# A graph-attention layer on one Trainium2 core: the first stage reordered, packing ahead of the first mask, the late h chunks between half pairs, V's first two chunks on GpSimd

## The reference

```
h      = relu(layernorm(x)) @ W.T + b_W
e      = leaky_relu((h @ a1)[:, None] + (h @ a2)[None, :] + b_a, slope 0.2)
scores = where(adj > 0, e, -9e15)
out    = x + softmax(scores, axis=1) @ h
```

## Time and profile before

| | |
|---|---|
| median of 3 runs | 202.64 us (202.4 to 202.82) |
| profiled execution, its span | 200.8 us |
| TensorE matmul busy | 194.9 us (97%), 3183 instructions |
| VectorE busy | 183.0 us (91%) |
| ScalarE busy | 147.9 us (74%) |
| GpSimd busy | 52.4 us (26%) |
| DMA | 75.66 MB, mean 377 GB/s |

### The profile page before, as it was taken

How to read it: one execution, slowest core, us unless ns; L and a number is a source line. 1 busy time by engine, 2 the same in 40 slices (tenths; PEclk the granted TensorE clock), 3 DMA queues, 4 the chain that set the end, 5 groups by cost and what they waited for, 6 DMA issues and landing times.

```text
span 200.8 us, 7230 instructions
## 1 busy us (share of the span) xinstructions
PE 194.9 (97%) x3183; PEld 189.2 (94%) x3183; DVE 183.0 (91%) x265; ACT 147.9 (74%) x192; POOL 52.4 (26%) x66
## 2 busy tenths in 40 slices
PE   7969999999999999999999999999999999999993
PEld 7648889999999999999999999999999999999993
DVE  4779999999998799897999999999999999999745
ACT  2679879898882777689988888899588888996000
POOL 1002479699995010205000000072000000510000
PEclk9999999999999999999999999999999999999999
DMA  5999999999999999999999999999999999997012
GB/s 181 376 417 418 407 403 423 421 418 415 422 432 408 418 423 419 416 421 418 415 419 423 419 418 421 421 411 421 419 418 418 415 421 416 418 383 226 6 43 66
DMA packets 15968, 75.66 MB, mean 377 GB/s; under 512 B 1600, under 2 KB 5952, under 8 KB 7616
## 3 DMA queue, kind: packets, MB, share of 16 engines
q1 hardware_dynamic: 15792, 75.06, 91.7%
q10 hardware_dynamic: 144, 0.13, 0.3%
HBM read 73.08 MB, written 2.11 MB: 374 GB/s over the span
## 4 chain that ended last, share of the span: by engine, by line
PE 91%; DMA 4%; SPq 1%; DVE 1%; issue 1%; POOL 0%
PE ps L836 29%; PE ps L834 29%; PE ps L840 29%; DMA adj_sb<-in_adj_t 4%; PE ps L808 2%; PE ps L798 2%; SPq L268 1%; SPq L273 1%; PE ps L876 1%; DVE mask L476 0%; POOL bad L788 0%; DVE rden L504 0%; DVE rg L510 0%; DVE bad L519 0%; DVE upper L576 0%
## 5 line engine op out<-in xcount | busy, mean ns | idle before, releaser
L834 PE MATMUL ps<-V,w 128*128 128x129 f16 x1024 | 174.3, 221 | 0.0
L836 PE MATMUL ps<-V,w 128*128 128x129 f16 x1024 | 174.3, 221 | 0.0
L840 PE MATMUL ps<-V,w 128*128 128x129 f16 x1024 | 174.3, 221 | 0.0
L379 ACT ACTIVATE mask<-adj_sb 128x1024 bf16<-128x1024 int32 x126 | 125.5, 1056 | 28.6 <-DMA adj_sb<-in_adj_t 28.6
L459 DVE SCALAR_TENSOR_TENSOR w<-g_row,pairs,mask 128x1024 f32<-128x1024 f32 x96 | 120.5, 1320 | 5.5 <-ACT mask L379 3.6
L834 PEld LDWEIGHTS ps<-V,w 128*128 128x128 f16 x1024 | 100.2, 98 | 1.5 <-ACT H L340 0.7
L836 PEld LDWEIGHTS ps<-V,w 128*128 128x128 f16 x1024 | 100.2, 98 | 1.0 <-issue 1.0
L840 PEld LDWEIGHTS ps<-V,w 128*128 128x128 f16 x1024 | 100.2, 98 | 0.0
L459 DVE SCALAR_TENSOR_TENSOR w<-ps,pairs,mask 128x1024 f32<-128x1024 f32 x31 | 37.4, 1267 | 0.0
L785 POOL TENSOR_TENSOR xT<-xT,x_sb 128x512 f32<-128x512 f32 x6 | 11.5, 1932 | 79.8 <-ACT xT L394 79.8
L739 POOL TENSOR_TENSOR x_sb<-x_sb,b_row 128x512 f32<-128x512 f32 x8 | 10.0, 1301 | 0.0
(11 more groups left out here) (93 smaller groups left out, 63.8 us busy)
## 6 DMA issues: line engine op xcount, KB each, us to landing
adj_sb<-in_adj_t SPq DMA_DIRECT2D x64, 1024.0 KB, 10.3
xT<-in_x_t SPq DMA_DIRECT2D x8, 256.0 KB, 7.5
x_sb<-in_x_p SPq DMA_DIRECT2D x3, 512.0 KB, 10.9
g_row<-g_dram SPq DMA_DIRECT2D x1, 1536.0 KB, 10.3
out<-xT SPq DMA_DIRECT2D x3, 512.0 KB, 9.9
x_sb<-in_x_p SPq DMA_DIRECT2D x2, 256.0 KB, 4.2
out<-xT SPq DMA_DIRECT2D x1, 192.0 KB, 3.4
out<-xT SPq DMA_DIRECT2D x3, 64.0 KB, 1.6
```

The lines of the kernel that those rows point to most:

```text
L379: nc.scalar.activation(mask[:, m % MASKS, r], adj_sb[:, m % HELD, r], ACT.Relu, scale=CONNECTED).then_inc(mask_ready, 1)
L834: nc.tensor.matmul(sums[:, bank, a, :], w16[:, m % SLOTS, col:col + P, 1], V[:, jt, 0, 0:NF], start=(jt == 0 and a == 0), stop=False, skip ...
L836: nc.tensor.matmul(sums[:, bank, a, :], w16[:, m % SLOTS, col:col + P, 1], V[:, jt, 1, 0:NF], start=False, stop=False, skip_group_check=True)
L840: last = nc.tensor.matmul(sums[:, bank, a, :], w16[:, m % SLOTS, col:col + P, 0], V[:, jt, 0, 0:NF], start=False, stop=(jt == NT - 1), ski ...
```

## The change

TensorE does the first three pairs in one go behind h chunk 3, then centring 4, and puts the late h chunks and centrings between half pairs of pairs 3 and 4. In the first pair all products with V's high part come before those with its low part. Within every pair the order of the three products of a block becomes high with high, low with high, high with low. ScalarE's and VectorE's lists are put in the matching order; VectorE packs ahead of the first mask and takes some statistics earlier, and no longer makes products or low parts of V. GpSimd makes the low part of V's chunk 0 (`lows`, in two halves, with the high part still by ScalarE's `highs`) and both parts of chunk 1 (`halves(1)`). Loads, their order and the centring are as before. The diff, cut to its core:

```diff
 # ScalarE
                 relu_chunk(3)
-                highs(0)
+                take_chunk(2)
+                highs(0, 2)
                 first_mask()
-                take_chunk(2)
+                highs(2, 4)
+                take_chunk(3)
                 mask_part(1)
-                take_chunk(3)
+                mask_part(2)
+                weights(1)
+                mask_part(3)
                 relu_chunk(4)
-                highs(1)
-                mask_part(2)
+                mask_part(4, (0,))
                 take_chunk(4)
                 relu_chunk(5)
-                weights(1)
-                mask_part(3)
+                mask_part(4, (1,))
                 take_chunk(5)
                 relu_chunk(6)
-                mask_part(4)
+                mask_part(5, (0,))
                 take_chunk(6)
                 relu_chunk(7)
-                mask_part(5)
+                mask_part(5, (1,))
                 take_chunk(7)
                 mask_part(6)
                 weights(2)
 # VectorE
-                early_mask()
+                statistics(2, 5, 8)
                 pack(0)
                 scale_weights(0)
-                products(0)
+                early_mask()
                 dve.wait_ge(pairs_ready, 1)
                 weigh_first(0)
-                lows(0)
                 weigh_first(1)
                 weigh(0, 1)
-                statistics(2, 5, 8)
+                statistics(3, 0, 4)
                 weigh(1, 0)
                 weigh(1, 1)
-                products(1)
-                lows(1)
                 scores(1)
                 weigh(2, 0)
                 weigh(2, 1)
+                statistics(3, 4, 8)
                 pack(1)
                 scale_weights(1)
-                statistics(3)
                 weigh(3, 0)
                 weigh(3, 1)
                 statistics(4)
 # GpSimd
+                def lows(g0, g1):
...
+                    step(nc.gpsimd.tensor_tensor(prod[:, 0, r, :], H[:, r, H0:HC], by, ALU.mult))
+                    pool.wait_ge(high_ready, g1 // 2)
+                    nc.gpsimd.tensor_tensor(V[:, r, 1, 0:NF], prod[:, 0, r, :], V[:, r, 0, 0:NF],
+                                            ALU.subtract).then_inc(low_ready, 1)
+
                 deviations(2, 3)
+                lows(0, 2)
+                lows(2, 4)
+                halves(1)
                 halves(2)
                 halves(3)
 # TensorE
+                def first_pair():
+                    pe.wait_ge(high_ready, 1)
+                    pe.wait_ge(w_begun, 1)
+                    for k in range(GI):
+                        if k == CT:
+                            pe.wait_ge(w_ready, 1)
+                        high_products(0, 0, k)
+                    pe.wait_ge(w_ready, 2)
+                    for k in range(GI):
+                        high_products(0, 1, k)
+                    pe.wait_ge(low_ready, 1)
+                    for side in range(2):
+                        for k in range(GI):
+                            last = low_product(0, side, k)
+                    last.then_inc(mm_done, 1)
...
                 h_chunk(3)
+
+                pe.wait_ge(h_ready, 3)
+                first_pair()
+                whole(1)
+                whole(2)
                 centre_chunk(4)
-
-                pe.wait_ge(h_ready, 3)
-                whole(0)
+                side_of(3, 0)
                 h_chunk(4)
                 centre_chunk(5)
-                whole(1)
+                side_of(3, 1)
                 h_chunk(5)
                 centre_chunk(6)
-                whole(2)
+                side_of(4, 0)
                 h_chunk(6)
                 centre_chunk(7)
-                whole(3)
+                side_of(4, 1)
                 h_chunk(7)
-                for m in range(4, NM - ENDS):
+                for m in range(5, NM - ENDS):
```

More of the change, by code:

```diff
@@ L211, in gat_layer_kernel @@
         ones_ready = sem("ones_ready")
-        product_ready = sem("product_ready")
         high_ready = sem("high_ready")
@@ L361, in weights, with highs, mask_part @@
                                          scale=SLOPE).then_inc(weights_ready, 1)
-                def highs(c):
+                def highs(g0, g1):
                     act.wait_ge(scaled_ready, 1)
                     act.wait_ge(ones_ready, 1)
-                    act.wait_ge(h_ready, c + 1)
-                    for j in range(CT):
-                        g = c * CT + j
+                    act.wait_ge(h_ready, 1)
+                    for g in range(g0, g1):
                         ins = nc.scalar.activation(V[:, g, 0, 0:NF], H[:, g, H0:HC], ACT.Copy, scale=evr[:, g:g + 1])
                     ins.then_inc(high_ready, 1)
-                def mask_part(m):
+                def mask_part(m, sides=(0, 1)):
                     act.wait_ge(adj_loaded[m % HELD], 16 * (m // HELD + 1))
-                    for side in range(2):
+                    for side in sides:
                         if m >= MASKS:
@@ L547, in statistics @@
                         last = nc.vector.bn_stats(stats[:, g, :], x_sb[:, g, :])
+                        if i >= FIRST_SETS and g % CT == CT - 1:
+                            last.then_inc(stats_ready, 1)
                     if i >= FIRST_SETS:
-                        if first + k1 == end:
-                            last.then_inc(stats_ready, 1)
                         return
@@ L586, in scale_weights @@
                     nc.vector.tensor_tensor(evr[:, r], ev[:, r], rstd[:, 2, r], ALU.mult).then_inc(scaled_ready, 1)
[L588 to L601, removed]
                 step_(nc.vector.memset(ramp[:, 0:1], 0.0))
@@ L719, in deviations @@
                     r = slice(SETS[first][0], SETS[end - 1][1])
-                    pool.wait_ge(stats_ready, end - FIRST_SETS)
+                    pool.wait_ge(stats_ready, SETS[end - 1][1] // CT - FIRST_SETS)
                     nc.gpsimd.tensor_tensor(spread[:, 0, r], stats[:, r, 2], stats[:, r, 5], ALU.add)
@@ L735, in add_b @@
                     else:
-                        pool.wait_ge(stats_ready, i - FIRST_SETS + 1)
+                        pool.wait_ge(stats_ready, SETS[i][1] // CT - FIRST_SETS)
                     pool.wait_ge(b_row_loaded, 16)
@@ L746, in halves @@
                     r = slice(c * CT + k0, c * CT + k1)
-                    part = 1 if c < 4 else 2
+                    part = 0 if c < 2 else 1 if c < 4 else 2
                     pool.wait_ge(scaled_ready, part + 1)
@@ L750, in halves @@
                     pool.wait_ge(h_ready, c + 1)
-                    if c < 4:
-                        pool.wait_ge(low_ready, c - 1)
                     by = evr[:, r].rearrange("p (n a) -> p n a", a=1).to_broadcast([P, k1 - k0, NF])
@@ L757, in halves @@
                                             ALU.subtract).then_inc(v_ready, 1)
+                def lows(g0, g1):
+                    r = slice(g0, g1)
+                    pool.wait_ge(scaled_ready, 1)
+                    pool.wait_ge(ones_ready, 1)
+                    pool.wait_ge(h_ready, 1)
+                    by = evr[:, r].rearrange("p (n a) -> p n a", a=1).to_broadcast([P, g1 - g0, NF])
+                    step(nc.gpsimd.tensor_tensor(prod[:, 0, r, :], H[:, r, H0:HC], by, ALU.mult))
+                    pool.wait_ge(high_ready, g1 // 2)
+                    nc.gpsimd.tensor_tensor(V[:, r, 1, 0:NF], prod[:, 0, r, :], V[:, r, 0, 0:NF],
+                                            ALU.subtract).then_inc(low_ready, 1)
                 deviations(2, 3)
+                lows(0, 2)
+                lows(2, 4)
+                halves(1)
                 halves(2)
@@ L811, in h_chunk, with high_products @@
                     last.then_inc(h_done, 1)
-                def products(m, k0, k1):
+                def high_products(m, side, k):
                     group, at = divmod(m, PAIRS)
+                    jt = 2 * at + side
+                    col = side * GC + k * P
+                    bank, a = sums_at(group, k)
+                    nc.tensor.matmul(sums[:, bank, a, :], w16[:, m % SLOTS, col:col + P, 1], V[:, jt, 0, 0:NF],
+                                     start=(jt == 0 and a == 0), stop=False, skip_group_check=True)
+                    return nc.tensor.matmul(sums[:, bank, a, :], w16[:, m % SLOTS, col:col + P, 0], V[:, jt, 0, 0:NF],
+                                            start=False, stop=False, skip_group_check=True)
@@ new lines, in low_product, with products @@
+                def low_product(m, side, k):
+                    group, at = divmod(m, PAIRS)
+                    jt = 2 * at + side
+                    col = side * GC + k * P
+                    bank, a = sums_at(group, k)
+                    return nc.tensor.matmul(sums[:, bank, a, :], w16[:, m % SLOTS, col:col + P, 1], V[:, jt, 1, 0:NF],
+                                            start=False, stop=(jt == NT - 1), skip_group_check=True)
```

(20 more changed lines are left out.)

## The result

The changed kernel takes 207.04 us (median of 4 runs, 206.77 to 207.62) against 202.52 us before, a ratio of 1.0227 (95% interval 1.0201 to 1.0252): 4.5 us slower. Forecast were 206.9 us. The profiled execution, 207.62 us with a span of 206.1, is the slowest of the four; the spans of the others are 205.2 to 205.5.

The account below looks back on a forecast made before the run. TensorE, dense from 16.89 us, was taken as the bound. Losses of 2.5 us at pair 3 and 1.75 at pairs 6 and 7 give 200.8 + 4.25 = 205.05 us of span, plus 1.84 makes 206.9 us; range 204.9 to 208.6.

Parts of the forecast that it names:

- The place: TensorE, dense from 16.89 us to its end, can win only ahead of that and loses every hole added behind.
- the new order of the products: Three products inside every pair: reordering costs 0, within 0.2 us either way, as each matmul had its own weight load.
- The front end: Ahead of the first product: packing 0.95 us earlier, first product at 15.0, at best 1.0 us won.
- Pairs 0 to 2: TensorE waits of 0.8 and 1.3 us, pair 2 at 22.65; all covered by the next wait, 1.5 to spare.
- Pair 3: Block 3's mask still starts at 25.29, so pair 3 starts at 27.72 and pair 5 at 39.5; 2.5 us lost.
- Pairs 6 and 7: Late take 7 delays mask(6); TensorE idles 0.4, 0.1 and 1.25 us, a second loss of 1.75 us.
- The total: Whole kernel: 4.25 us lost, 205.05 us of span plus 1.84 to the median, 206.9 us; chance 0.62.
- the 1.84 from span to time: Time around the span: 202.64 - 200.8 = 1.84 us up to the median of the runs, added to the forecast span.
- (a): Rival: only pair 3's wait costs, the 1.75 at pairs 6 and 7 goes; 205.1 us, chance 0.16.
- (b): Rival: clock falls to 1.2 GHz in or behind 15 to 28 us; 209.6 us, chance 0.13 including other longer holes.
- (c): Rival: early start kept through centring chunk 4, reached at 24.0; gain 1.0 us, 201.6 us, chance 0.06.

Follow-up runs that it names:

- e_front: The changed kernel with its new front end kept and the late chunks put back between pairs 0 to 3 as before; 202.51 us, ratio 1.0012.
- e_late: The kernel before, with its own front end and only the late order of the change on TensorE and ScalarE; 207.71 us, ratio 1.0262.
- e_block3: The changed kernel with block 3's load moved ahead of x transposed 6, x set 4 and x transposed 7; 206.24 us.
- c_after: The changed kernel once more, unaltered; 206.93 us, ratio 1.0259 against the kernel before.
- e_mask6: The changed kernel with pair 6's first mask half before take 7, pair 7's mask before weights(2), packing part 2 behind pair 7's weights; 205.69 us.
- e_front2: New front end, late chunks as before, relu 6 before block 3's mask, relu 7 inside mask 4, pair 7's weights before packing part 2; 202.14 us.
- e_front2b: The same kernel as e_front2, run again unaltered; 202.28 us against 202.31 for the kernel before, ratio 1.0.

## Why the prediction was right

**The place.** The step on which it rests held: TensorE is the bound; from its first product on it idles only before 28.7 and before pairs 6 and 7, and it is dense behind, at 56.6 ns a matmul as before, so the new order of the products costs nothing that can be seen. e_front and e_late take the change apart into two halves, and the loss goes with the late order alone. What feeds pair 3 last is block 3 in the changed kernel (e_block3) and VectorE's list in e_late.

**The front end.** First product forecast at 15.0, found at 15.05; packing and GpSimd's first deviations 12.4, both found at 12.37. It holds for an execution whose first matmuls are quick, as they happened to be in both first profiles; in c_after the first product is at 16.00. That these vary I had not seen, as one trace of before does not show it. It costs the forecast nothing, since block 3 covers it.

**Pairs 0 to 2.** Side 1 of pair 0 at 16.7 (16.71), pair 1 at 19.8 (20.09), pair 2 at 22.65 (23.74, and 23.42 in c_after). Pair 2 is late because block 2's mask started at 21.22 and not at 20.2, and in c_after because it started at 20.54 and VectorE's scores took 0.5 more than in the first profile. GpSimd's first low part made one hole that I had not priced (0.26). All of it is absorbed, as said, with 1.15 and 0.84 idle before pair 3 where 1.5 was forecast.

**Pair 3.** ScalarE's wait for block 3 was forecast as some 2.5, and is 2.36 and 2.40. Pair 3 was forecast at 27.72; 28.68 with block 3's mask at 26.16, 28.05 with it at 25.52 (before: 25.29). From the mask on the sum is right to 0.1: 28.05 - 25.52 = 2.53 against 2.43. From pair 3 to pair 5 11.77 were forecast and 11.80 are found in both profiles.

**Pairs 6 and 7.** Holes of 0.4, 0.1 and 1.25 were forecast. In c_after pair 6 starts 0.5 late and pair 7 another 1.33 (47.12 - 39.85 = 7.27 for two pairs of 2.715), 1.83 in all against 1.75. e_mask6 shows the cause: with masks and packing moved, both holes go, and 206.93 becomes 205.69 (in another job, with the kernel before at 202.34 and not 202.23).

**The total.** A loss of 4.25 was forecast; 4.5 was measured, and 4.7 in the later job. In c_after pair 8 can start at 49.84 (47.12 + 2.715), 0.44 behind the forecast. Of this 0.23 is block 3's landing, taken from one execution; 0.1 lies between its mask and pair 3, the rest in the late pairs. That 206.9 and 207.04 agree to 0.14 is partly luck. The four spans have a median of 205.45, 0.4 above the 205.05 of the sum. The 1.84 from span to time was 0.2 to 0.3 too much, the other way: it was taken between a median of three runs and the span of one execution, and every execution with both numbers here shows 1.5 to 1.7 (207.62 - 206.1 = 1.5).

**The rivals.** (a), only pair 3's wait, falls with the holes before pair 7. (b), the clock, falls: 1.00 in all windows through 3.7 us of holes, so waits of this size did not take it down. (c), the early start kept, is what e_front and e_front2 come to with the filler back, and even there nothing of it can be measured.

One thing more speaks from the page: the DMA's rate drops to 324 GB/s from 40.5 to 50.5 (418 in that window before), since loads wait for the late masks: 23.4 us of waits of SyncE's queue for ScalarE's masks from 28 to 52, against 16.5 before. It costs nothing, as TensorE is dense from 50.5 to the end.

## What to carry to other kernels

Work that the bound engine must do anyway is worth most where its feed is still on the way: ahead of moving filler behind a stream, ask of each load in the stream when it lands, and add up what stands in front of it. A gain at the start of the chain is real only up to the next thing that lands by its own clock. And a wait that looks like waste in one profile may be cover for something that varies between executions.

## What the runs showed of the hardware

The first centring (two matmuls of 128 × 512 in f32) took 1.10 to 1.15 us in six of the ten traces and 1.83 to 2.06 in the other four, with the same work ahead of it. Shown by itself, the first of the two takes 1.20 in those four and 0.72 in e_front2, where a later one takes 0.59. In e_front2b the second centring took 1.80 too, against 1.02 in the other nine. The first product moved with them, by 2 us between the two executions of one kernel. The granted clock reads 1.00 from 4.7 to 8.0 in all of them, as in this window of e_front2b, so the rows do not say why.

```profile
4.70:8.00 3.30, 3.30 (x11) 2.19 (x11) 1.25 (x8) 0.62 (x3) 0.00 (x0) 1.00 1.01 295
```

The Trainium skill (TensorE: Matmul & The Clock Gate, What's actually happening) says that the moment at which the clock is let up to full speed at the start differs from run to run; matmuls at twice their time would fit it, but no run here shows it, as the granted clock reads 1.00.

Block 2 is in by 20.2 to 20.6 in some executions and at 21.2 to 21.4 in others (ScalarE's wait for it), with the same loads issued ahead of it.
